# Layer 4: taking part of a row maximum off VectorE, in 96 of 512 steps, with max(a, b) = b + relu(a - b)

## The reference

```python
q = split_heads(query @ Wq.T + bq)
k = split_heads(key @ Wk.T + bk)
v = split_heads(value @ Wv.T + bv)
scores = jnp.einsum('bhqd,bhkd->bhqk', q, k) / np.sqrt(HEAD_DIM)
weights = jax.nn.softmax(scores, axis=-1)
out = jnp.einsum('bhqk,bhkd->bhqd', weights, v)
```

## Time and profile before

| | us |
|---|---|
| median of 3 runs | 1950.11 |
| lowest, highest | 1945.99, 1951.56 |
| the profiled execution | 1962.35 |
| its span | 1960.5 |
| layer 4, from the first reduction of the steps to the last | about 1091 to 1751 |
| TensorE busy in the span | 1770.9 |
| VectorE busy | 1448.9 |
| ScalarE busy | 1170.1 |
| GpSimd busy | 374.3 |

### The profile page before, as it was taken

How to read it: one execution, slowest core, us unless ns; L and a number is a source line. 1 busy time by engine, 2 the same in 40 slices (tenths; PEclk the granted TensorE clock), 3 DMA queues, 4 the chain that set the end, 5 groups by cost and what they waited for, 6 DMA issues and landing times. The chain is left out here.

```text
span 1960.5 us, 32709 instructions
## 1 busy us (share of the span) xinstructions
PE 1770.9 (90%) x12524; PEld 1214.6 (62%) x12524; DVE 1448.9 (74%) x1675; ACT 1170.1 (60%) x2098; POOL 374.3 (19%) x250
## 2 busy tenths in 40 slices
PE   7988998989989967999988799999999999998865
PEld 5767777467757745878776455555555555555524
DVE  7637552587898855565665599999999998994575
ACT  1332333577777734353531388888888887894373
POOL 4223200144445412232312000010010000001000
PEclk8999998999999987999989699999999998998887
DMA  9798862158949841122226745655657645610000
GB/s 359 295 323 302 314 233 71 43 202 291 321 168 318 308 140 43 68 70 68 70 36 119 157 92 112 124 114 112 118 98 127 117 94 112 109 39 6 1 0 22
DMA packets 171815, 280.05 MB, mean 143 GB/s; under 512 B 21598, under 2 KB 100478, under 8 KB 164494
## 3 DMA queue, kind: packets, MB, share of 16 engines
q1 hardware_dynamic: 169934, 277.48, 50.1%
q10 hardware_dynamic: 1728, 0.49, 0.1%
HBM read 187.33 MB, written 88.14 MB: 141 GB/s over the span
## 5 line engine op out<-in xcount | busy, mean ns | idle before, releaser
L2314 DVE TENSOR_REDUCE xn_peaks<-psum 128x2 f32<-128x1024 f32 x512 | 621.5, 1224 | 53.7 <-PE psum L2113 46.0
L2269 ACT ACTIVATE moe_mix_transposed<-psum 128x512 f32<-128x512 f32 x1024 | 552.8, 597 | 91.2 <-PE psum L2118 52.1
L2118 PE MATMUL psum<-xn_q_stack,xn_k_words 50*128 50x256 f32 x2048 | 383.3, 311 | 15.8 <-ACT xn_q_whole L2243 9.6
L2118 PEld LDWEIGHTS psum<-xn_q_stack,xn_k_words 50*128 50x128 f32 x2048 | 254.3, 190 | 223.1 <-ACT moe_mix_transposed L2269 192.0
L2113 PE MATMUL psum<-xn_k_words,xn_q_stack 50*128 50x512 f32 x1024 | 377.9, 456 | 5.5 <-DMA xn_q_stack<-q_rows 3.4
L2150 PE MATMUL psum<-moe_mix_transposed,xn_v 128*32 128x256 f32 x4096 | 334.7, 399 | 2.0 <-issue 0.3
L2113 PEld LDWEIGHTS psum<-xn_k_words,xn_q_stack 50*128 50x128 f32 x1024 | 188.6, 188 | 13.3 <-DVE xn_peaks L2314 7.8
L931 POOL TENSOR_TENSOR mx_state<-mx_du,mx_b_all_channels 128x1024 f32<-128x1024 f32 x64 | 153.5, 2399 | 198.7 <-ACT mx_b_all_channels L1108 85.5
L1189 DVE TENSOR_TENSOR_SCAN mx_state<-psum,mx_state 128x1024 f32<-128x1024 f32 x64 | 146.2, 2285 | 50.8 <-ACT psum L1118 43.3
L322 PE MATMUL psum<-xw_ctx_natural,xw_weights_transposed 128*128 128x256 f32 x512 | 125.9, 392 | 15.4 <-DVE xw_weights_transposed L474 15.2
L2150 PEld LDWEIGHTS psum<-moe_mix_transposed,xn_v 128*32 128x32 f32 x4096 | 82.5, 109 | 75.0 <-issue 11.1
(11 more groups left out here) (347 smaller groups left out, 2563.2 us busy)
## 6 DMA issues: line engine op xcount, KB each, us to landing
xn_k_words<-k_words SPq DMA_DIRECT2D x384, 128.0 KB, 6.6
ctx_words<-xw_ctx_transposed_words SPq DMA_DIRECT2D x64, 512.0 KB, 7.2
ctx_chunk_words<-ctx_words SPq DMA_DIRECT2D x64, 512.0 KB, 5.6
k_words<-ctx_k_words SPq DMA_DIRECT2D x128, 256.0 KB, 2.6
v_all<-ctx_v SPq DMA_DIRECT2D x32, 544.0 KB, 3.4
xn_v<-v_all SPq DMA_DIRECT2D x32, 544.0 KB, 4.9
xw_mask<-in_mask_BxSxS_ik SPq DMA_DIRECT2D x8, 2048.0 KB, 7.9
xw_ctx_natural<-in_ctx SPq DMA_DIRECT2D x32, 512.0 KB, 6.7
```

The costliest lines, as they stand in the source:

```text
L2118: return pe.matmul(PS[:, narrow_bank("exp", n, step, a), half * S:(half + 1) * S], K[n % XN_KSLOTS][narrow_rows(a), kt * P:(kt + 1) * P], ...
L2269: act.activation(t["weights"][:, step % 4, a, :, :], bank.rearrange("p (t s) -> p t s", t=2), ACT.Exp, scale=XN_SCALE).then_inc(s.taken, 1)
L2314: dve.tensor_reduce(t["peaks"][:, m % 2, q, :, c], PS[:, 2 * (x % 2):2 * (x % 2) + 2, :], AX.X, ALU.max).then_inc(s.top_read, 1)
```

## The change

In every fourth step (x % 4 == 2) of pairs 2 to 7 of each batch, 96 of 512, the maximum over 512 keys is taken in another way. The keys of the chunk are halved into b (the first 256) and a (the last 256). TensorE makes b in one half of the bank, and in the other a - b: the product of the queries with a's keys, and on top of it that of the negated queries with b's keys. ScalarE takes relu(a - b) of both heads out of PSUM into SBUF, in one instruction behind both exponentials of the step. VectorE adds b to it and takes the maximum over the 256 sums, one instruction for each head. GpSimd makes the negated queries once for each batch, of the first 128 queries (these x always belong to the first query tile). Some buffers change places: the sums lie in a free part of the mixer's tile, the reciprocals in the place of the normed input, the relu's output in that of its transpose.

```diff
+XN_LIFT_EVERY, XN_LIFT_AT, XN_LIFTS = 4, 2, 2
+XN_LOWEST = -3.0e38
+def narrow_lifted(x):
+    return x >= XN_TOP + XN_LEAD and x // XN_TOP % XN_PAIRS >= 2 and x % XN_LIFT_EVERY == XN_LIFT_AT
...
+    t["lift"] = k.YT[:, :, 0:2 * S].rearrange("p i (a s) -> p i a s", a=2)
...
 # narrow_pool
+    def minus(b, earlier, done):
+        pool.wait_ge(earlier, done)
+        pool.wait_ge(s.q_in, 96 * (b + 1))
+        pool.wait_ge(s.zeros, 2 * (b + 1))
+        if b:
+            pool.wait_ge(s.top, 2 * XN_TOP * XN_PAIRS * b)
+        for a in range(2):
+            rows = narrow_rows(a)
+            pool.tensor_scalar(t["minus"][rows, :, :], t["Q"][rows, b % 2, :, 0:P].bitcast(F32), -1.0, None, ALU.mult
+                               ).then_inc(s.minus, 1)
+            pool.wait_ge(s.minus, 2 * b + a + 1)
...
             pool.tensor_tensor(t["row"][:], t["row"][:], t["bo"][:], ALU.add).then_inc(s.row, 1)
+            minus(0, s.row, 1)
         if n + 1 < XN_N:
             words(n + 1)
+        if n % XN_PAIRS == XN_PAIRS - 2 and n // XN_PAIRS < B - 1:
+            minus(n // XN_PAIRS + 1, s.words, 2 * (n + 2))
...
 # narrow_pe, maxima_ready
+        if i == 0 and m % XN_PAIRS == 2:
+            pe.wait_ge(s.minus, 2 * (m // XN_PAIRS + 1))
 # narrow_pe, maxima
-        return pe.matmul(PS[:, 2 * (x % 2) + a, :], Q[narrow_rows(a), m // XN_PAIRS % 2, m % XN_PAIRS, q * P:(q + 1) * P],
-                         K[m % XN_KSLOTS][narrow_rows(a), c * BANK:(c + 1) * BANK], start=True, stop=True)
+        queries = Q[narrow_rows(a), m // XN_PAIRS % 2, m % XN_PAIRS, q * P:(q + 1) * P]
+        keys_of = K[m % XN_KSLOTS][narrow_rows(a), c * BANK:(c + 1) * BANK]
+        if not narrow_lifted(x):
+            return pe.matmul(PS[:, 2 * (x % 2) + a, :], queries, keys_of, start=True, stop=True)
+        negated = t["minus"][narrow_rows(a), m % XN_PAIRS, :]
+        pe.matmul(PS[:, 2 * (x % 2) + a, 0:S], queries, keys_of[:, 0:S], start=True, stop=True)
+        pe.matmul(PS[:, 2 * (x % 2) + a, S:], queries, keys_of[:, S:], start=True, stop=False)
+        return pe.matmul(PS[:, 2 * (x % 2) + a, S:], negated, keys_of[:, 0:S], start=False, stop=True)
...
 # narrow_act
+    def lifted(x):
+        i = XN_LIFT_OF[x]
+        act.wait_ge(s.top, 2 * (x + 1))
+        if i >= XN_LIFTS:
+            act.wait_ge(s.top_read, XN_LIFTED[i - XN_LIFTS] + 1)
+        act.activation(t["lift"][:, i % XN_LIFTS, :, :], PS[:, 2 * (x % 2):2 * (x % 2) + 2, S:], ACT.Relu).then_inc(s.lift, 1)
...
             for a in range(2):
                 exponentials(n, step, a)
+            if XN_STEPS * n + step + XN_TOP + XN_LEAD in XN_LIFT_OF:
+                lifted(XN_STEPS * n + step + XN_TOP + XN_LEAD)
...
 # narrow_dve, maxima
         dve.wait_ge(s.top, 2 * (x + 1))
+        if narrow_lifted(x):
+            i = XN_LIFT_OF[x]
+            dve.wait_ge(s.lift, i + 1)
+            for a in range(2):
+                last = dve.tensor_tensor_reduce(t["lift"][:, i % XN_LIFTS, a, :], PS[:, 2 * (x % 2) + a, 0:S],
+                                                t["lift"][:, i % XN_LIFTS, a, :], 1.0, XN_LOWEST, ALU.add, ALU.max,
+                                                t["peaks"][:, m % 2, q, a, c:c + 1])
+            last.then_inc(s.top_read, 1)
+            return
         dve.tensor_reduce(t["peaks"][:, m % 2, q, :, c], PS[:, 2 * (x % 2):2 * (x % 2) + 2, :], AX.X, ALU.max
                           ).then_inc(s.top_read, 1)
```

More of the change, by code:

```diff
@@ L1745 @@
 XN_LATE = 24 * S
+XN_LIFT_EVERY, XN_LIFT_AT, XN_LIFTS = 4, 2, 2
+XN_LOWEST = -3.0e38
+def narrow_lifted(x):
+    return x >= XN_TOP + XN_LEAD and x // XN_TOP % XN_PAIRS >= 2 and x % XN_LIFT_EVERY == XN_LIFT_AT
+XN_LIFTED = [x for x in range(XN_N * XN_TOP) if narrow_lifted(x)]
+XN_LIFT_OF = {x: i for i, x in enumerate(XN_LIFTED)}
 def narrow_mix_bank(i):
@@ L1792, in narrow_tiles @@
          "row": sb("row_constant", [P, D]), "qx": sb("q_whole", [P, KD, S]), "qw": sb("q_words", [P, 2, KD, S], F32R),
-         "Q": sb("q_stack", [P, 2, XN_PAIRS, S], F32R),
+         "Q": sb("q_stack", [P, 2, XN_PAIRS, S], F32R), "minus": sb("q_minus", [P, XN_PAIRS, P], F32R),
          "K": [k.xn_keys] + [sb(f"k_words{i}", [P, S2]) for i in range(1, XN_KSLOTS)], "V": sb("v", [P, 2, XN_KT * 2 * XN_VW + XN_VPAD]),
@@ L1796, in narrow_tiles @@
          "neg": sb("neg_max", [P, 2, QT * 2]), "neg_words": sb("neg_words", [P, QT, 2, XN_HALF], F32R),
-         "choice": sb("choice", [P, 2, 2, XN_DH]), "ident": sb("identity_words", [P, P], F32R), "sums": sb("sums", [P, 2, S]),
-         "den": sb("denominators", [P, 2, S // XN_SPREAD]), "rsum": sb("rsum_by_channels", [P, KD, S])}
+         "choice": sb("choice", [P, 2, 2, XN_DH]), "ident": sb("identity_words", [P, P], F32R), "den": sb("denominators", [P, 2, S // XN_SPREAD]), "rsum": k.Y[:, 0:KD, :]}
+    t["lift"] = k.YT[:, :, 0:2 * S].rearrange("p i (a s) -> p i a s", a=2)
     late = k.moe_mixT[:].rearrange("p e s -> p (e s)")
@@ L1803, in narrow_tiles @@
     t["OT"] = late[:, 20 * S:22 * S].rearrange("p (c s) -> p c s", c=KD)
+    t["sums"] = late[:, XN_LATE + FFN_W_SIZE:XN_LATE + FFN_W_SIZE + 2 * S].rearrange("p (i s) -> p i s", i=2)
     t["proj"] = late[:, 22 * S:24 * S].rearrange("p (q d) -> p q d", q=QT)
@@ L1811, in narrow_sems @@
                      "neg words sum acc o_in den_in r_out r_in halves den ident o wide row plus x "
-                     "choice chosen last_den last_o last_pe")
+                     "choice chosen last_den last_o last_pe minus lift")
     return s, [k.xn_keys_in] + [k.sem_row(f"xn_keys{slot}_", XN_KHALVES) for slot in range(1, XN_KSLOTS)], k.sem_row("xn_values", 2)
```

## The result

The kernel after takes 2019.68 us, median of 4 runs (2012.91 to 2022.48), beside 1950.66 us before (4 runs, 1945.99 to 1951.56). The ratio is 1.0357, with a 95% interval of 1.0337 to 1.0377: slower by 69 us. Forecast were 2022 us, with a range of 1980 to 2068.

The account below looks back on a forecast made before the run. The prediction took TensorE to bound layer 4. Its terms, 68 us for stalled pairs, 4 for the rest and 0, gave +72 us, so 2022 us from the 1950.11 us median, range 1980 to 2068 us.

Parts of the forecast that it names:

- The reading of the bound: Layer 4: bound by TensorE at 1.233 us a step, VectorE 7% behind, ScalarE further off.
- Item 1: TensorE in a lifted step: exponential matmuls held back behind the other half's triple, +0.24 us, +23 us over 96.
- Item 2: ScalarE in a lifted step: relu behind both exponentials, from 1.68 to 2.28 us, with room for it.
- Item 3: VectorE in a lifted step: two add-and-maximum operations take 0.88 us, bounds 0.76 and 1.29, replacing a 1.23 us reduction.
- Item 4: Second step behind a lift: TensorE stands 0.60 us for VectorE behind the relu; four steps take 5.78 instead of 4.93.
- Item 5: Pairs with lifts: stalls absorb the shift and the wait for the copy; a pair becomes 23.12 us, +68 over 24.
- Item 6: Batch outputs on VectorE, GpSimd's negation, moved buffers, half clock: +4 us in all, from VectorE's output work.
- The sum against the profiled execution: Whole kernel: +72 us on the profiled 1962.35 us gives about 2034 us.
- A: Lifted steps: only TensorE's matmuls count, +23 us, 1973 us; chance 0.10.
- B: Lifted steps on VectorE: the add-and-maximum pair is slow at 1.29 us, total 2062 us; chance 0.12.
- C: Layer 4: VectorE is the true bound, so the change saves 33 us, 1917 us; chance 0.04.
- D: TensorE's clock: 0.6 us pauses make it fall more often, six falls +30 us, 2052 us; chance 0.06.

Follow-up runs that it names:

- e4: Kernel before, with VectorE's reductions in the 96 steps over 512 elements instead of 1024; ratio to the kernel before 1.0002 (0.9985 to 1.0018).
- e2: Kernel after with TensorE's matmuls and VectorE's two new operations, but no relu and no wait for one; 1961.32 us, ratio to the kernel before 1.0082.
- e1: Kernel after with TensorE's new matmuls alone: no relu, VectorE reduces all 1024 elements as before; 1955.54 us, ratio to the kernel before 1.0058.
- e8: Kernel after with TensorE and VectorE as before the change, ScalarE doing an unused SBUF-to-SBUF relu at the 96 places; 1960.21 us, ratio 1.0073.
- e3: Kernel after with the relu between the two exponentials of its step instead of behind both; 1983.41 us, ratio to the kernel before 1.0203.
- e5: Kernel after with the relu and its wait kept, but the old 1024-element reduction behind it; 2059.23 us, ratio to the kernel before 1.0582.
- e6: Kernel after with one lift in a pair instead of four, that of step 12 just ahead of the shift; ratio to the kernel before 1.0051.

## Why the prediction was right, point by point

**The reading of the bound** held: TensorE bound layer 4 (e4, e2), and the 19.60 of 20.28 on VectorE was no limit.

**Item 1, TensorE,** was mis-sized: 0.24 us a lift forecast, 0.12 measured (e1: 0.50 a pair, 12 us instead of 23). The step that failed is that the exponential matmuls are held back in program order behind the triple of the other half. The earlier trace rows fitted that reading and the other one alike. The timeline after shows the third maxima matmul of one half (L2150) starting at 1407.74, together with the first (L2148) of the other, although an exponential matmul (started at 1407.86) stands between them in the program. Each half of the rows makes its five matmuls of 256 columns, 0.12 apart behind the second, one more 0.12 than before, and starts none of them late for the other half. The results are another matter. The exponential of a = 0 needs the matmuls at 1407.39 and 1407.62, and the second ends at 1407.90; ScalarE, idle for 0.27 us, begins at 1408.09. That is 0.07 behind the end of the other half's L2150 (1407.74 + 0.28), which stands ahead of that second matmul in the program. At 95 lifts it is 0.07 behind that and 0.19 behind its own matmul; in the kernel before, the usual distance from its own is 0.07. By these rows, whose matmul ends are modelled, TensorE starts matmuls out of program order across the halves but hands over their results in order.

**Item 2, ScalarE:** the relu starts at 1.67 and ends at 2.27 behind the first load; forecast were 1.68 and 2.28. The 0.12 by which the exponentials were to begin later did come, at 0.70, though the matmuls weren't held back: by the rows under item 1 their results were. The sum came out right here by a step that was half wrong. No table load appeared between exponentials. e8 shows the engine's room: 0.63 us of work at each lift costs 0.13 us on average.

**Item 3, VectorE:** the pair of operations takes 0.78 us, not 0.88, close to the lower bound of 0.76. Each is 0.42 long and the second starts 0.35 behind the first. The accumulator's read is an instruction of its own, 0.083 us. That such an operation is two instructions is what the Trainium skill states (VectorE: DVE Perf Modes, "Two Vector instructions with no wait between them"), and the trace agrees. By these rows the read adds nothing to the pair but at its end, since it starts together with the next operation.

**Item 4, the wait,** is the mechanism, and it stands: e3 moved the relu 0.49 us forward and a steady cycle fell by that, e5 lengthened what follows the relu by 0.41 and the cycle rose by that. The way from the relu to VectorE takes 0.14 us, not 0.04. The new operation waits for two semaphores, but that this is the reason is not shown. From VectorE's end to the load it takes 0.07 at half of the lifts and 0.12 at the others; forecast was 0.11. Terms of +0.10, -0.10 and 0 or -0.05 nearly cancel: the cycle was forecast at 5.78, and a quarter of the pair is 5.79. That this agrees so closely is luck; the mechanism is not. VectorE's wait for the relu was to be "1.2 us or so" and is 1.56; it counts from the end of the reduction ahead of the lift, which comes at 0.79. TensorE's 0.12 too much made no difference here, since the stall takes what TensorE leaves: 0.67 instead of 0.60.

**Item 5, what the stall hides:** right: the shift and the copy cost nothing beside the stalls (e6; in the kernel after the step with the copy is 1.27 us, 1.36 before). What it left out is a new 0.07 in the step ahead of the lift of step 12. VectorE's last stage of the maxima follows a lift there, its next reduction ends at 1401.44, and the load that should come at 1401.52 comes at 1401.56, the first matmul 0.07 late. A pair was forecast at 23.12 and is 23.17.

**Item 6, the rest,** +4 us, all but failed to come. The first two lifted pairs of the three later batches take 149.4 us after (25.30 and 24.01 in the second batch) and 131.4 in e4: 18.0 more, where six times the regular 2.89 gives 17.3. The step that failed is to count VectorE's work for a batch's output in full "in a chain through VectorE"; VectorE has 1.6 us idle at each lift, in which it probably finds room. No run tests that.

**The sum against the profiled execution** was 2034 us, and it took 2022.48. From the first to the last L2321 the kernel before needed 669.1 us with 14 us at half clock in them, e4, whose regular pairs are the same, 657.8 with the clock at 1.00 from 1123.7 to 1740, and the kernel after 726.7. Against e4 the kernel after is 68.9 us longer. Of the 11 us between the kernel before and e4, 5.8 are the pair with the stretch at half clock (27.12 us instead of 21.36 for its like), which the trace after lacks. Another 3.0 lie in the first pair, where the mean clock from 1112 to 1124 was 0.51 in the kernel before and 0.75 in e4; the other 2.5 are spread over the second pair and pairs at a batch's start. That the forecast started from the median, not from the profiled execution, kept this out.

**The rivals.** A: e1 is what it describes, at half its price; it fell. B: the pair of operations is 0.78, not 1.29; it fell, and e5 shows that its way of counting was right. C fell with e4. D: the clock stayed at 1.00 from 1123.7 to 1720 through 80 lifts with stalls of 0.67 to 0.72 us, 5.8 us apart within a pair. The Trainium skill (TensorE: Matmul & The Clock Gate, "A second HAM failure mode: psum-queue depth-cycling") describes pauses of that kind as lowering the clock; the trace does not show it for pauses of this length and spacing.

## What to carry to other kernels

Before work is moved off an engine that looks full, take away about as much of that engine's work alone: here 11% less in a pair was worth nothing (e4), because the other full engine was the bound. A step that gives a result to a third engine in the middle of a two-deep buffer is priced by that buffer's deadline. Add up the queue ahead of the new instruction, the instruction, and all that must follow before the buffer is free. Here TensorE's own next use of the banks was at 2.59 (1.36 + 1.23), the relu ended at 2.27 and 0.99 had still to follow it; the 0.67 that is missing is the stall. Where such a stall exists, small waits that fall into it become free: here a lift that costs 0.89 us alone costs 0.44 beside the shift.

## What the runs showed of the hardware

- Matmuls in different halves of TensorE's rows did not start in the program's order: one began 0.12 us ahead of another that stands before it. Behind the second, those of 256 columns in each half followed at 0.12 us. Their results were handed over in program order: at 95 lifts ScalarE began 0.07 us behind the end of the other half's third matmul and 0.19 behind its own.
- An operation that waits for a ScalarE result and for the scores began 0.14 us behind the relu's end with the add-and-maximum and 0.11 with the reduction. A reduction that waits for scores alone began 0.04 behind them. TensorE's load began 0.07 us behind VectorE's end at two of the four lifts of a pair and 0.12 at the others.
- The add-and-maximum over 256 elements, one operand in PSUM and one in SBUF, takes 0.42 us, as the plain two-source operation does.
- A relu over 128x512 takes 0.605 us from PSUM and 0.63 from SBUF to SBUF (e8), with no table load between exponentials.
